# Stacks read from two queues, an output bias added a stage earlier, and filler products on TensorE in a four-layer transformer kernel

## The chip, the cores and the metric

The kernel runs on one core of a Trainium2 chip, as one launch. The metric is the device time in microseconds; 963.40, 967.69 and 969.59 us were measured for the kernel before, so its median is 967.69 us. One execution was also profiled. It took 962.79 us, 961.0 us of them in the span of the profile.

A core has five engines that run their own instruction streams: TensorE (PE; its weight loads are shown as PEld), VectorE (DVE), ScalarE (ACT), GpSimd (POOL) and SyncE (SP). Here SP issues nearly all transfers. The profile also lists the clock that was granted to TensorE, as a share of full speed.

## The reference

1,024 tokens of width 256 pass through four layers. Each layer normalises and adds an attention-like part, then normalises and adds a feed-forward part. All inputs and weights are float32.

```python
x = x + L0_attn(ln(x))      # 16 heads of 16: q, k scaled, rotary, LN; causal softmax; @ Wo + bo
x = x + L0_ffn(ln(x))       # W2 (fwht(silu(x W1) * (x W3))), hidden width 1024
x = x + L1_attn(ln(x))      # 16 heads of 16, biases, causal softmax; @ WO + b
x = x + L1_ffn(ln(x))       # silu(gate) * up, the 2 largest of every 4 kept, down
x = x + L2_attn(ln(x))      # sigmoid gates, tanh values, h[t] = g[t] h[t-1] + v[t]
x = x + L2_ffn(ln(x))       # 8 experts, the best 2 of each token, and a shared expert
x = x + L3_attn(ln(x))      # attention over an axis of few keys; @ wo
x = x + L3_ffn(ln(x))       # ternary weights, silu(gate) * up, RMS norm, down
```

## The kernel before, in words

The tokens lie in 8 tiles of 128 in `m.x` (128 partitions, tile, 256). The program is a row of stages. Each stage is a block of its own with one instruction stream per engine and its own semaphores, and between two stages all five engines meet at a barrier. The stages in order, by the tag in the names of their tiles, with their rough start in the profiled execution: n0 (norm), rotary, s0 (58 us), at0 (79), o0 (216), f0 (237), n2 (318), s1 (328), at1 (352), o1 (490), f1 (507), n4 (601), recurrence (612), n5 (631), f2 (640, experts), n6 (842), single key (850), o3 (878) and f3 (891).

**Norms.** `norm_stage` (L99) computes mean and deviation per tile on VectorE and ScalarE, and TensorE transposes each normalised tile by two products with the identity (L253), each pair waiting for its tile. The transposed halves are copied out of PSUM by ScalarE and VectorE, for n2 and n4 as a high and a low part (L220, L179), for n5 and n6 plain (L224, L183). For n0 the stage waits first for the identity (`ident_ready`). The feed-forward stages f0, f1 and f3 have their norm inside: `HalfNorm` (L1294) turns the first four tiles (`turn`, L1359) ahead of the first products (L1472; in f1 those of `sparse_ffn_stage`), and the other four later.

**Split stage.** q and k must reach the scores as three bf16 parts that stand under each other on the partitions. `split_stage` (L413) makes the parts by units (ScalarE and VectorE), computes V on TensorE (L450) and lets VectorE add V's bias for all 8 tiles on the way into `v_all` (L489). Once a unit is done SP writes it to `scratch` in HBM (L497; semaphore `written[u]`), and `read_stack` (L402) reads it back 16 partitions by 16: six transfers of `qs` for w = 0, six of `ks` for w = 1, all on `m.stacked`. There are four groups of four heads; SP reads group 0 in the split stage, and groups 1 to 3 within the attention (`read_group`).

**Attention.** `attention_stage` (L649) computes in TensorE's products of L705 and L708 (mask) the scores whose maxima VectorE takes (L806), sends the negated maxima as three extra rows into the stack, computes the scores anew, less their maximum (L729), lets ScalarE take the exponential (L786) and multiplies by the values (L745). `order_of_products` (L559) plans, from constants for each engine's speed, in which order TensorE does maxima, scores and values; the result is the list `ORDER`, the same for both attentions. The first entry of kind "values" is number 39 of it, counted from 0.

**Output stage.** `out_stage` (L855) turns `oT` back (L882), takes the reciprocal of the softmax sums (L940), normalises (L942), transposes again (L892), multiplies by the output weights (L900) and adds into `m.x` (L947). At its start VectorE adds the output bias to all of `m.x` (L951) and waits for that. o0 computes, besides, products with a Hadamard matrix for f0's weights. `single_key_stage` (L1937) does projections and transposes on TensorE, then softmax and sums on VectorE into `att`.

**Experts.** f2 opens with 32 gate products of 8 columns (L1038), then come products of the shared expert (L1066) while VectorE sorts out the routing. GpSimd sends the tokens to their slots with 16 indirect transfers (L1285).

## Time and profile before

| | |
|---|---|
| median of 3 runs | 967.69 us (963.40 to 969.59) |
| profiled execution | 962.79 us, span 961.0 us |
| mean granted clock of TensorE | 0.901 |
| PE busy | 797.6 us, 83% of the span (4306 instructions) |
| DVE busy | 624.4 us, 65% (1318) |
| ACT busy | 387.0 us, 40% (655) |
| POOL busy | 153.4 us, 16% (208) |
| moved by DMA | 63.96 MB, mean 67 GB/s |
| costliest groups | maxima of the scores, L806 on DVE: 90.7 us in each attention; exponentials, L786 on ACT: 73.8 us in each |

Busy is time in which an instruction of the engine runs; waiting at a semaphore is idle. A row of the timeline gives the start and the busy time of an instruction (or of several of one kind that follow each other), what it reads and writes, and in brackets how long its engine had been idle before it and what it waited for. "<-PEq L112" means that the engine's own sequencer came last, here at the barrier between stages; "issue" means that no wait is to be seen. Two clocks matter: 1.00 is TensorE at 2.4 GHz, 0.50 at 1.2 GHz.

### The profile page before, as it was taken

How to read it: one execution, taken by the hardware profiler on the slowest of the kernel's cores; microseconds unless marked ns; L12 is line 12 of the kernel's file. 1: busy time of each engine (PE TensorE's matmuls, PEld its weight loads, DVE VectorE, ACT ScalarE, POOL GpSimd, SP SyncE). 2: the span in 40 equal slices, each digit the busy share in tenths (PEclk: the TensorE clock that was granted, in tenths of full speed). 3: DMA queues.
4: the chain of work that ended last, by engine and by line, in shares of the span. 5: the costliest groups of instructions: out<-in, count | busy, mean ns of one | idle time of the engine just before them, and what ended most of it. 6: DMA issues, size and time to landing. Idle time of an engine off the chain costs nothing. (4 is left out here: it accounts for less than half of the span.)

```text
span 961.0 us, 12407 instructions
## 1 busy us (share of the span) xinstructions
PE 797.6 (83%) x4306; PEld 513.8 (53%) x4306; DVE 624.4 (65%) x1318; ACT 387.0 (40%) x655; POOL 153.4 (16%) x208
## 2 busy tenths in 40 slices
PE   6256899987899678999986896669999999478796
PEld 5143344325688553334255786555556666266575
DVE  6887888808774689788346977452267771265764
ACT  3141457683521423666746432541122222043543
POOL 1800121120020001112210000105112221100143
PEclk9666899999899787999998997769999999888798
DMA  6227300000000472200007000993201110310000
GB/s 206 93 81 217 103 2 1 3 2 1 1 1 1 147 246 84 67 3 2 2 1 127 1 1 1 326 375 113 66 28 45 45 45 27 109 45 1 1 23 22
DMA packets 49554, 63.96 MB, mean 67 GB/s; under 512 B 12534, under 2 KB 34806, under 8 KB 49494
## 3 DMA queue, kind: packets, MB, share of 16 engines
q1 hardware_dynamic: 47622, 58.05, 19.7%
q0 software_dynamic: 1872, 5.13, 1.5%
q8 instruction: 35, 0.57, 0.3%
q14 instruction: 25, 0.20, 0.1%
HBM read 50.30 MB, written 15.51 MB: 68 GB/s over the span
## 5 line engine op out<-in xcount | busy, mean ns | idle before, releaser
L806 DVE TENSOR_REDUCE at1mx<-at1ps_s 128x1 f32<-128x512 f32 (+3 forms) x152 | 90.7, 655 | 17.5 <-PE at1ps_s L708 10.4
L806 DVE TENSOR_REDUCE at0mx<-at0ps_s 128x1 f32<-128x512 f32 (+3 forms) x152 | 90.7, 655 | 17.0 <-PE at0ps_s L708 10.0
L786 ACT ACTIVATE at1probs<-at1ps_e 128x1024 f32<-128x1024 f32 (+3 forms) x96 | 73.8, 809 | 45.9 <-PE at1ps_e L729 45.5
L786 ACT ACTIVATE at0probs<-at0ps_e 128x1024 f32<-128x1024 f32 (+3 forms) x96 | 73.8, 809 | 45.5 <-PE at0ps_e L729 45.2
L1070 PE MATMUL f2ps<-gu_raw,f2xT_b 128*128 x184 | 82.9, 593 | 1.0 <-ACT f2xT_b L1145 1.0
L1163 ACT ACTIVATE f2sg<-f2ps 128x512 f32<-128x512 f32 x31 | 18.5, 598 | 134.3 <-PE f2ps L1070 100.9
L705 PE MATMUL at0ps_s<-ks,qs 96*128 96x512 bf16 (+3 forms) x192 | 58.1, 364 | 6.8 <-DMA ks<-scratch 5.3
L705 PE MATMUL at1ps_s<-ks,qs 96*128 96x512 bf16 (+3 forms) x192 | 58.0, 363 | 6.0 <-DMA ks<-scratch 4.4
L1239 DVE TENSOR_TENSOR f2h<-f2sg,f2ps 128x512 f32<-128x512 f32 x31 | 21.3, 686 | 61.6 <-ACT f2sg L1163 42.1
L1070 PEld LDWEIGHTS f2ps<-gu_raw,f2xT_b 128*128 128x128 f32 x184 | 34.8, 190 | 35.5 <-issue 34.4
L729 PE MATMUL at1ps_e<-qs,ks 99*128 99x512 bf16 (+3 forms) x192 | 46.7, 339 | 4.1 <-ACT at1probs L786 2.3
L729 PE MATMUL at0ps_e<-qs,ks 99*128 99x512 bf16 (+3 forms) x192 | 46.7, 339 | 3.9 <-ACT at0probs L786 1.8
L1290 POOL DMA_INDIRECT rows_out<-xT,f2x_in x23 | 29.0, 1259 | 124.8 <-DVE xT L1227 124.8
L795 POOL TENSOR_SCALAR_AFFINE_SELECT at0probs<-at0probs 128x256 f32<-128x256 f32 x64 | 25.8, 409 | 143.0 <-ACT at0probs L786 142.5
L795 POOL TENSOR_SCALAR_AFFINE_SELECT at1probs<-at1probs 128x256 f32<-128x256 f32 x64 | 25.8, 409 | 140.7 <-ACT at1probs L786 140.2
L1098 PE MATMUL f2ps<-dn_raw,xT 128*128 x184 | 43.7, 380 | 1.1 <-DVE xT L1227 1.1
L745 PE MATMUL at0ps_v<-at0probs,v_all 128*32 128x512 f32 (+3 forms) x384 | 41.8, 498 | 0.1
L745 PE MATMUL at1ps_v<-at1probs,v_all 128*32 128x512 f32 (+3 forms) x384 | 41.8, 498 | 0.1
L705 PEld LDWEIGHTS at0ps_s<-ks,qs 96*128 96x128 bf16 x192 | 18.9, 104 | 43.0 <-DVE at0mx L806 28.3
L705 PEld LDWEIGHTS at1ps_s<-ks,qs 96*128 96x128 bf16 x192 | 18.9, 105 | 42.1 <-DVE at1mx L806 28.2
L1098 PEld LDWEIGHTS f2ps<-dn_raw,xT 128*128 128x128 f32 x184 | 33.2, 190 | 5.3 <-issue 1.7
L1708 PE MATMUL f1ps_o<-f1part_dn,f1hpart 128*128 128x256 f32 x192 | 27.7, 312 | 6.5 <-DVE f1hpart L1835 6.5
(400 smaller groups left out, 1772.1 us busy)
## 6 DMA issues: line engine op xcount, KB each, us to landing
gu_raw<-in_L_ffn_w_gate_up SPq DMA_DIRECT2D x8, 1024.0 KB, 12.4
scratch<-parts SPq DMA_DIRECT2D x8, 768.0 KB, 3.8
qs<-scratch SPq DMA_DIRECT2D x48, 128.0 KB, 2.8
ks<-scratch SPq DMA_DIRECT2D x48, 128.0 KB, 2.8
dn_raw<-in_L_ffn_w_down SPq DMA_DIRECT2D x8, 512.0 KB, 12.2
f2x_in<-slots_in SPq DMA_DIRECT2D x23, 129.0 KB, 2.0
slots_in<-in_c_empty SPq DMA_DIRECT2D x1, 2944.0 KB, 17.2
traw<-in_L_ffn_w_gate_up SPq DMA_DIRECT2D x1, 2048.0 KB, 11.6
```

What stands on the lines that cost most here:

```text
L705: ins = pe.matmul(ps_s[:, i % MAX_BANKS, a:a + width], qs[0:STK, g, j + h, qt * P:qt * P + P], ks[0:STK, g, j + h, lo:lo + width], start=T ...
L729: ins = pe.matmul(ps_e[:, v % SCORE_PAIRS, i, 0:n], ks[0:ROWS, g, j, kt * P:kt * P + P], qs[0:ROWS, g, j, lo:lo + n], start=True, stop=True)
L745: ins = pe.matmul(ps_v[32 * j:32 * j + 32, CH - n:CH], v_all[:, g, kt, j, :], probs[:, (s * GH + j) % PROBS, 0:n], start=(kt == 0), stop=( ...
L786: act.activation(probs[:, slots(v), 0:n], ps_e[:, v % SCORE_PAIRS, :, 0:n], ACT.Exp, scale=HD ** -0.5)\
L795: pool.affine_select(pair, pair, [[0, PAIR], [1, P]], ALU.is_ge, 0.0, base=0, channel_multiplier=-1)\
L806: dve.tensor_reduce(mx[:, p % 2, lo // CH, j:j + heads, t], rows_of, AX.X, ALU.max).then_inc(s_red, 1)
L1070: ins = pe.matmul(o, xT_b[:, a % 2, k, :], w, start=(k == 0), stop=(k == KD - 1))
L1098: ins = pe.matmul(ps[:, 6, 0:D], hT[:, b % 2, f, :], w, start=(f == 0), stop=(f == FT - 1))
L1163: act.activation(sg[:, u % 2, :], ps[:, u % 2, :], ACT.Silu).then_inc(sgs, 1)
L1239: dve.tensor_tensor(h[:, u % 2, :], sg[:, u % 2, :], ps[:, 2 + u % 2, :], ALU.mult).then_inc(hs, 1)
L1290: pool.indirect_dma_start(ys[:, :], bass.IndirectOffsetOnAxis(ap=dest, axis=0), y[:, b % YS, :], None)\
L1708: ins = pe.matmul(ps_o[:, c % 2, t, :], hpart[:, a, j, t * P:t * P + P], parts[1][wp][:, blk * 4 + j, :], start=(blk == 0 and j == 0 and t ...
```

## The change

1. **Fillers.** A new `keep_busy` issues `count` bf16 products of the identity by the identity repeated four times (128 x 512) into a PSUM bank that is not in use then; nothing reads them. They stand ahead of and behind the transposes of n2, n4, n5 and n6 (9 and 8), ahead of and behind those of the first half norm in f0, f1 and f3 (9 and 8), at the start of both attentions (6, and one ahead of each of the first 39 entries of `ORDER`), and at the end of the single-key stage (12).
2. **Stack transfers.** Of group 0, SP reads the six of `qs` and two of `ks`; GpSimd reads the other four of `ks`, on a semaphore of their own, both after `written[1]`.
3. **V bias.** For tiles 4 to 7 a product of one row (ones by bias) adds it on TensorE and ScalarE copies the result; VectorE keeps tiles 0 to 3.
4. **Output bias.** VectorE adds it at the end of the attention, not at the start of the output stage.

```diff
+def keep_busy(pe, m, bank, count):
+    for _ in range(count):
+        pe.matmul(bank.rearrange("p (a n) -> p a n", n=P), m.identb[:], m.identb[:].unsqueeze(1).to_broadcast([P, CH // P, P]),
+                  start=True, stop=True)
...
@@ norm_stage, tensor
             if ident_ready is not None:
                 pe.wait_ge(*ident_ready)
+            else:
+                keep_busy(pe, m, ps[:, 7, :], 9)
...
+            if ident_ready is None:
+                keep_busy(pe, m, ps[:, 7, :], 8)
@@ read_stack
-def read_stack(sp, m, g, w):
-    for slot, part in enumerate(PARTS_OF[w]):
+def read_stack(eng, m, g, w, slots=range(NSLOT), signal=None):
+    for slot in slots:
+        part = PARTS_OF[w][slot]
         src = m.scratch[w, part, g * GH * HD:(g + 1) * GH * HD, :].rearrange("(h d) n -> d h n", d=HD)
-        sp.dma_start(m.stacks[w][slot:STK:NSLOT, g, :, :], src).then_inc(m.stacked, 16)
+        eng.dma_start(m.stacks[w][slot:STK:NSLOT, g, :, :], src).then_inc(m.stacked if signal is None else signal, 16)
+BY_SP = 2
+def stacked_by_sp(g):
+    return (g + 1) * STACK_SIGNALS - 16 * (NSLOT - BY_SP)
@@ split_stage
-                                    start=start, stop=stop)
+                                    start=start, stop=stop and t < T // 2)
+                if t >= T // 2:
+                    ins = pe.matmul(ps[:, t, 0:D], m.ones[0:1, :].to_broadcast([1, P]), v_bias[0:1, :],
+                                    start=False, stop=True)
...
+            for t in range(T // 2, T):
+                act.wait_ge(v_full, t + 1)
+                act.activation(v_all[:, :, t, :, 0:HD], heads(ps[:, t, 0:D]), ACT.Copy)
...
-            for t in range(T):
+            for t in range(T // 2):
                 dve.wait_ge(v_full, t + 1)
                 dve.tensor_tensor(v_all[:, :, t, :, 0:HD], heads(ps[:, t, 0:D]), heads(v_bias), ALU.add)
...
-            for w in range(2):
-                sp.wait_ge(m.written[w], 16)
-                read_stack(sp, m, 0, w)
+            sp.wait_ge(m.written[0], 16)
+            read_stack(sp, m, 0, 0)
+            sp.wait_ge(m.written[1], 16)
+            read_stack(sp, m, 0, 1, range(BY_SP))
...
+        @block.gpsimd
+        def _(pool):
+            pool.wait_ge(m.written[1], 16)
+            read_stack(pool, m, 0, 1, range(BY_SP, NSLOT), m.stacked_by_pool)
@@ attention_stage
-                    pe.wait_ge(m.stacked, (g + 1) * STACK_SIGNALS)
+                    pe.wait_ge(m.stacked, stacked_by_sp(g))
+                    pe.wait_ge(m.stacked_by_pool, 16 * (NSLOT - BY_SP))
...
+            keep_busy(pe, m, ps_v[:], 6)
             pe.wait_ge(m.stacked_ones, 16)
-            for kind, n in ORDER:
+            for place_in_order, (kind, n) in enumerate(ORDER):
+                if place_in_order < FIRST_VALUES:
+                    keep_busy(pe, m, ps_v[:], 1)
...
+            dve.tensor_tensor(m.x[:], m.x[:], out_bias.unsqueeze(1).to_broadcast([P, T, D]), ALU.add)
@@ out_stage
-            if bias is not None:
-                b = bias.unsqueeze(1).to_broadcast([P, T, D])
-                dve.tensor_tensor(m.x[:], m.x[:], b, ALU.add).then_inc(biased, 1)
-                dve.wait_ge(biased, 1)
@@ HalfNorm.turn
         if half:
             pe.wait_ge(self.ready, KD)
+        else:
+            keep_busy(pe, m, self.spare, 9)
...
         ins.then_inc(self.turned, 1)
+        if not half:
+            keep_busy(pe, m, self.spare, 8)
@@ single_key_stage
+            pe.wait_ge(copied, len(blocks))
+            keep_busy(pe, m, ps_b[:, 0, :].bitcast(F32), 12)
```

TensorE at the opening of at0, before (L705 scores for the maxima, L708 the mask):

```order
L686 UNCONDITIONAL_BRANCH [waits barrier_Pool_Activation_PE_DVE_SP_release]
L705 MATMUL at0ps_s<-ks,qs 128x128 [waits stacked0,stacked_ones0]
L708 MATMUL at0ps_s<-identb,above 128x128
L705 MATMUL at0ps_s<-ks,qs 128x128
...
L705 MATMUL at0ps_s<-ks,qs 128x256
```

and of the change (L78 is the filler, L738 the product that was L705, L741 the mask):

```order
L718 UNCONDITIONAL_BRANCH [waits barrier_Pool_Activation_PE_DVE_SP_release]
L78 MATMUL at0ps_v<-identb 128x512 x6
L78 MATMUL at0ps_v<-identb 128x512 [waits stacked_ones0]
L738 MATMUL at0ps_s<-ks,qs 128x128 [waits stacked_by_pool0,stacked0]
L741 MATMUL at0ps_s<-identb,above 128x128
...
L78 MATMUL at0ps_v<-identb 128x512
L738 MATMUL at0ps_s<-ks,qs 128x256
```

Seven fillers stand ahead of the first scores, the first six of them ahead of any wait of the stage, and one ahead of each further entry.

SP in s0, before (`written0_1` is `written[1]` of layer 0, `s0_low` counts finished parts):

```order
L497 DMA scratch<-parts 128x3x1024 [waits s0_low] x2
L406 DMA qs<-scratch 16x4x1024 [waits written0_0]
L406 DMA qs<-scratch 16x4x1024 x5
L406 DMA ks<-scratch 16x4x1024 [waits written0_1]
L406 DMA ks<-scratch 16x4x1024 x5
```

and of the change, SP first, then GpSimd:

```order
L522 DMA scratch<-parts 128x3x1024 [waits s0_low] x2
L418 DMA qs<-scratch 16x4x1024 [waits written0_0]
L418 DMA qs<-scratch 16x4x1024 x5
L418 DMA ks<-scratch 16x4x1024 [waits written0_1]
L418 DMA ks<-scratch 16x4x1024
```

```order
L98 ISA x10
L536 UNCONDITIONAL_BRANCH
L418 DMA ks<-scratch 16x4x1024 [waits written0_1]
L418 DMA ks<-scratch 16x4x1024 x3
L442 UNCONDITIONAL_BRANCH
```

Four of the six transfers of `ks` have moved from SP's stream to GpSimd's, which had no work in this stage; the two writes that follow on SP come four issues earlier.

## Rows read from the trace of the kernel before

PE and PEld are TensorE's products and weight loads; in every timeline the columns are those that the group of f0 names.

**Rows 1.** The page, part 2: the granted clock in 40 slices, in tenths.

```profile
PEclk9666899999899787999998997769999999888798
```

**Rows 2.** Stretches: length, busy (count) of PE, PEld, DVE, ACT, POOL, clock, DMA share, GB/s.

```profile
58.30:64.10 5.80, 5.79 (x28) 5.80 (x29) 3.76 (x8) 4.04 (x6) 0.00 (x0) 0.50 0.13 17
64.10:66.00 1.90, 1.90 (x13) 1.75 (x13) 1.87 (x5) 1.48 (x3) 0.00 (x0) 1.00 0.23 77
79.00:84.60 5.60, 5.60 (x31) 3.12 (x32) 4.57 (x9) 0.00 (x0) 0.00 (x0) 0.50 1.00 316
84.60:88.00 3.40, 1.48 (x8) 0.42 (x6) 3.23 (x10) 0.36 (x2) 0.00 (x0) 1.00 0.92 236
88.00:98.20 10.20, 9.54 (x34) 4.15 (x35) 8.66 (x15) 3.24 (x3) 0.82 (x2) 0.50 0.47 146
245.30:248.40 3.10, 3.03 (x7) 2.50 (x8) 2.04 (x9) 1.78 (x4) 0.00 (x0) 0.50 0.00 0
328.20:333.70 5.50, 5.49 (x13) 4.34 (x14) 1.12 (x2) 0.69 (x1) 0.00 (x0) 0.50 0.72 222
334.00:341.50 7.50, 7.50 (x34) 6.03 (x33) 6.93 (x13) 6.23 (x11) 0.00 (x0) 1.00 0.32 110
494.20:497.60 3.40, 3.40 (x12) 2.86 (x11) 1.30 (x4) 0.47 (x2) 0.00 (x0) 0.50 0.00 0
612.20:617.00 4.80, 4.77 (x11) 3.80 (x12) 0.00 (x0) 1.96 (x2) 0.00 (x0) 0.50 1.04 389
878.40:883.20 4.80, 4.69 (x14) 3.59 (x15) 0.42 (x1) 1.15 (x3) 0.00 (x0) 0.50 0.00 0
898.60:903.70 5.10, 5.07 (x16) 4.22 (x17) 1.68 (x6) 2.13 (x5) 0.00 (x0) 0.50 0.00 0
```

**Rows 3.** Timeline, f0: start, length, engine, line, operation, count, [idle before <-releaser].

```profile
241.38 1.85 PE L1359 MATMUL f0ps_o<-ident,n1xn 128*128 128x128 f32 x8 [4.66 <-DVE n1xn L1340]
...
245.37 0.77 PE L1472 MATMUL f0ps_g<-x1hi,f0part_gu 128*128 128x512 f32 x1 [2.15 <-DVE x1lo L1371]
```

**Rows 4.** Timeline, behind the norm n2 and in the norm n6.

```profile
328.21 0.77 PE L440 MATMUL s1ps<-x2hi,wp1hi 128*128 128x512 f32 x1 [2.05 <-PEq L112]
845.13 1.11 PE L253 MATMUL n6ps<-ident,n6xn 128*128 128x128 f32 x4 [17.18 <-DVE n6xn L163]
```

**Rows 5.** Timeline, opening of the MoE stage f2.

```profile
639.56 6.97 PE L1038 MATMUL f2ps<-gate_w,xT 128*128 128x8 f32 x32 [1.03 <-PEq L112]
...
646.38 6.07 PE L1066 MATMUL f2ps<-xT,shared_gu 128*128 128x512 f32 x8
```

**Rows 6.** Timeline, opening of the output stage o3.

```profile
878.46 1.08 PE L892 MATMUL o3ps<-ident,att 128*128 128x128 f32 x4 [4.13 <-PEq L1944]
```

**Rows 7.** Timeline, opening of the output stage o1.

```profile
489.67 2.29 DVE L951 TENSOR_TENSOR x<-x,l1b 128x2048 f32<-128x2048 f32 x1 [22.82 <-PEq L664]
...
492.77 0.44 PE L892 MATMUL o1ps<-ident,o1a_tm 128*128 128x128 f32 x2 [2.03 <-DVE o1a_tm L942]
```

**Rows 8.** Timeline of s0's end and the opening of at0; SPq is SP's DMA queue.

```profile
64.75 3.69 SPq L497 DMA_DIRECT2D scratch<-parts  x2
...
73.10 3.78 SPq L406 DMA_DIRECT2D ks<-scratch  x6
73.75 2.73 DVE L489 TENSOR_TENSOR v_all<-s0ps,l0b 128x256 f32<-128x256 f32 x8
...
78.98 0.27 PE L705 MATMUL at0ps_s<-ks,qs 96*128 96x128 bf16 x1 [5.35 <-DMA ks<-scratch]
```

**Rows 9.** Instructions of line L1285: count, min/median/max ns, first and last start.

```profile
L1285 POOL DMA_INDIRECT slots_in<-xn,f2slot_i x16: 957/961/1174, 655.8 to 675.0; - x16
```

**Rows 10.** The page, parts 5 and 6: busy, mean ns; KB, us to landing.

```profile
L1290 POOL DMA_INDIRECT rows_out<-xT,f2x_in x23 | 29.0, 1259 | 124.8 <-DVE xT L1227 124.8
...
scratch<-parts SPq DMA_DIRECT2D x8, 768.0 KB, 3.8
```

**Rows 11.** Timeline of VectorE in the first scores of at0.

```profile
93.57 3.17 DVE L806 TENSOR_REDUCE at0mx<-at0ps_s 128x1 f32<-128x512 f32 x5 [1.04 <-PE at0ps_s L705]
```

More of the change, by code:

```diff
@@ L854, in out_stage @@
 @stage
-def out_stage(nc, ctx, m, tag, w, w_ready, bias, oT=None, att=None, turned=None):
-    names = ("_tr1", "_norm", "_tr2", "_aT", "_mm", "_res", "_rz", "_had_mm", "_had_b", "_had_v", "_biased")
-    tr1, norm, tr2, aT_s, mm, res, rzs, had_mm, had_b, had_v, biased = (sem(nc, ctx, tag + x) for x in names)
+def out_stage(nc, ctx, m, tag, w, w_ready, oT=None, att=None, turned=None):
+    names = ("_tr1", "_norm", "_tr2", "_aT", "_mm", "_res", "_rz", "_had_mm", "_had_b", "_had_v")
+    tr1, norm, tr2, aT_s, mm, res, rzs, had_mm, had_b, had_v = (sem(nc, ctx, tag + x) for x in names)
     with ExitStack() as tmp:
@@ L1294, with __init__ @@
 class HalfNorm:
-    def __init__(self, nc, own, tmp, tag, room):
+    def __init__(self, nc, own, tmp, tag, room, spare):
         names = ("_sums", "_stats", "_std", "_inv", "_shift", "_xn_v", "_xn_a", "_tr", "_high", "_ready")
@@ L1309, in __init__ @@
         self.warm = sb("warm", [P, 1])
-        self.room = room
+        self.room, self.spare = room, spare
     def tiles(self, half):
@@ L1689, in sparse_ffn_stage @@
         ps_o = tmp.enter_context(nc.psum_tensor(tag + "ps_o", [P, 2, TC, D], F32))
-        nm = HalfNorm(nc, ctx, tmp, norm, ps_o[:, 1].rearrange("p (k t) d -> p k (t d)", k=KD))
+        nm = HalfNorm(nc, ctx, tmp, norm, ps_o[:, 1].rearrange("p (k t) d -> p k (t d)", k=KD), ps_u[:, 1, :])
         block = tmp.enter_context(nc.Block())
@@ L2158, in attention @@
             oT = sb("oT" + layer, [P, GROUPS, N], stack=stack)
-            attention_stage(nc, ctx, m, "at" + layer, v_all, oT)
-            out_stage(nc, ctx, m, "o" + layer, wa[:, :, 3 * D:4 * D], ready, bias, oT=oT, turned=turned)
+            attention_stage(nc, ctx, m, "at" + layer, v_all, oT, bias)
+            out_stage(nc, ctx, m, "o" + layer, wa[:, :, 3 * D:4 * D], ready, oT=oT, turned=turned)
         with ExitStack() as ffn0:
```

12 lines of the change are left out of this document (7 added, 5 removed).

## The prediction, as it stood before the result was known

> **What bounds the kernel now.** I first read the busy shares in 40 slices with the granted clock of TensorE. It is often below full speed, and nearly always where a stage opens [rows 1]. Then I took a table of stretches with their granted clock [rows 2]. Nine stretches show TensorE busy almost without a gap at 0.50, the lower of its two levels (1.2 GHz), and each follows a stretch in which TensorE paused for some microseconds. The price of the low level comes from one stage: in s1 13 products of 512 columns took 5.50 us at 0.50 (0.42 us each), and 34 took 7.50 us at 1.00 (0.22 us). So a stretch in which TensorE is the bound and works at 0.50 gives back about 0.45 of its length at 1.00. Third, the timeline at each edited place says what ends the wait there, and fourth, the rows of the stack transfers say when an attention can begin.
>
> **The change part by part.** One filler is a bf16 product of 128 by 512 columns, so by the s1 pace 0.42 us at the low and 0.22 us at the full clock. There are 9 before and 8 behind the transposes in n2, n4, n5, n6 and in the first half norms of f0, f1, f3; 6 plus 39 in each attention; 12 at the end of the single-key stage: 68 + 51 + 90 + 12 = 221. That is 49 us of new work on TensorE at full clock, 93 us at the low one. It costs nothing where TensorE would wait anyway, so the cover has to be checked place by place.
>
> *Half norms.* In f0 TensorE waited 4.66 us for the first normalised tile; 9 fillers take 2.0 us (low: 3.8), so they fit either way. Eight transposes end at 243.2, the first product starts 2.15 later, at 245.37 [rows 3]: 8 fillers take 1.8 us at the full clock and fit, at the low clock they take 3.4 and make it 1.2 us late. If the clock holds, the 3.1 us at 0.50 that follow [rows 2] give 1.4 us; the first activation waits for them and comes that much earlier. f1 is the same code: 1.4. f3 needs 5.1 us at 0.50: 2.3.
>
> *Full norms.* n2's transposes end 2.05 us before the next stage's first product, which starts at 328.21, released by the barrier [rows 4]. Eight fillers fit (1.8 us in 2.05), and what hides them is the copies out of PSUM on ScalarE and VectorE. s1 then starts at the full clock; its 5.5 us at 0.50 give 2.4. n4 has the same shape, and the recurrence spends 4.8 us at 0.50: 2.2. In n5 and n6 there is less to copy: the gap behind n5's transposes is 1.03 us [rows 5], and n6 has the same code. Eight fillers overrun it by 0.7 at the full clock and by 2.4 at the low one. In n5 the transposes themselves end some tenths earlier at a higher clock, so I take 0.5. n6 comes when TensorE has been idle for 17.18 us [rows 4], so its 9 fillers ahead run at the low clock; I take 0.7 lost. Behind n5 stand 32 gate products of 8 columns, 6.97 us, and then 8 products of 512 columns, 6.07 us [rows 5]. The gate products at the full clock save 3.1. During those 6.97 us of short products the clock did not rise, so I do not count on it to hold through them, and take nothing for the second group (at best 0.45 of it, 2.7 more).
>
> *Single-key stage.* TensorE is done 4.13 us before its next stage starts at 878.46 [rows 6]; 12 fillers take 2.6 us there (low: 5.0, 0.9 late). The output stage spends 4.8 us at 0.50: 2.2.
>
> *Output bias.* The addition of 2048 elements takes 2.29 us. In o1 it stands first, and the first normalisation waits for it: TensorE waits 2.03 us until 492.77 [rows 7]. At the end of the attention VectorE had been idle for 22.82 us, so there it is free. The reciprocal needs the first two tiles' transposes (some 0.7 us of the stage), not the addition: 1.6 saved. In o0 TensorE first multiplies by the Hadamard matrix, which does not need x and hides the addition: 0. With that gap gone the clock should not fall in o1; the 3.4 us at 0.50 give 1.5.
>
> *V bias.* VectorE loses 4 of 8 additions (0.34 us each, 2.73 in all [rows 8]), ScalarE gains four copies, TensorE four one-row products (by the s1 pace 0.42 us each at most). All of it is done before the transfers are: 0. If they were faster, up to 1.4 would show.
>
> *Stack transfers.* SP issues 6 of ks in 3.78 us (0.63 each) behind 6 of qs, the last at 76.2, and the first product of at0 waits for it until 78.98: it lands 2.7 after its issue [rows 8]. GpSimd now sends four of them. The trace has no plain transfer from GpSimd; its 16 indirect ones of L1285 stand 1.28 us apart (0.96 busy) [rows 9], and the 23 of L1290, beside a busier VectorE, are 1.26 busy [rows 10], so about 1.6 apart. Both queues wait for written[1]: its write was issued at about 68.1 (the second of two, done at 68.4 [rows 8]) and such writes land after 3.8 [rows 10], so 71.9 (SP came to it at 73.1 and did not wait). At SP's pace the last of GpSimd's would land at 76.5, 2.5 before now, and SP's own two at 76.4; at 1.28 the last is issued at 75.7 and lands at 78.4, 0.6 earlier; at 1.6 at 79.4, 0.4 later. I take 0.6, the nearest row, per attention.
>
> *Fillers in the attention.* From 79.0 to 98.2 VectorE's maxima set the pace: the longest of its waits for TensorE there is 1.04 us [rows 11]. With the first maximum some 0.4 earlier, a clock that holds gives at most 1.9 in all. TensorE's own work in these 19.2 us was 5.60 + 1.48 + 9.54 = 16.6 us busy, 15.1 of them at 0.50; at the full clock it is half of those and 1.5, 9.1 us, and 39 fillers add 8.6. That is 17.7 in 19.2, but only if the clock is high: each microsecond at 0.50 does half. From 3 us at 0.50 on, the attention can get longer. I take 0.5 saved per attention (bounds: 1.9 saved, 13.8 lost).
>
> **Sum:** 1.4 + 1.4 + 2.3 + 2.4 + 2.2 + 3.1 + 2.2 + 1.6 + 1.5 + 2 × 0.6 + 2 × 0.5 = 20.3 saved, less 0.5 + 0.7: 19.1. The profiled execution took 962.8 us (span 961.0), so 943.7. The three timed runs have their median at 967.7, so against them it is 948.6; the lowest of them was 963.4. I forecast **946**, 2.3 above the sum on the profiled execution, and put the rivals on the same scale.
>
> **A rule against the trace.** From 58.3 to 64.1 TensorE ran nothing but fp32 transposes, 5.79 us busy at 0.50, and from 64.1 it had 1.00 [rows 2]. The Trainium skill, page "TensorE: Matmul & The Clock Gate", section Part 4, says that transposes do not count as activity for the clock gate. The trace disagrees; by that rule the clock would sink in every norm between the two groups of fillers, and the sum would lose what rival A takes away.
>
> **Rivals.** *A. The clock sinks again inside the norms.* For: the tiles arrive slowly, so TensorE is idle for most of the time between the 9 and the 8; against: the fillers behind come at once. Then s1, the recurrence and the gate products keep the low clock for most of their stretch: 19.1 - 7.7 = 11.4 saved, **954**. Chance 0.22.
> *B. GpSimd's transfers are starved.* For: VectorE works almost without a gap there, and GpSimd's transfers beside a busy VectorE took a third longer. If none got out before VectorE ends (75.1 with four additions instead of eight), the last would land at 75.1 + 3 × 1.28 + 2.7 = 81.6, 2.7 late in both attentions in place of 0.6 early: 19.1 - 6.6 = 12.5 saved, **953**. Chance 0.08. The Trainium skill, page "SBUF — State Buffer", section "SBUF: two separate sides", describes this as a trap: GpSimd cannot write descriptors while VectorE holds the shared port.
> *C. Slower: the fillers do not lift the clock.* They are on the order list in front of work, not behind it. If the clock stays at 0.50 in both openings, 39 × 0.42 = 16.4 us stand beside the 16.6 us of own work in 19.2: 13.8 longer each. The other sites then save nothing but 1.6 (bias) and 1.2 (stack), and lose 1.4 at n2, 2 × 2.4 at n5 and n6, and about 4 × 1.2 at the half norms and the single-key stage: 962.8 + 27.6 + 11.0 - 2.8 = 998.6, on the runs' scale **1001**. It decides from 3 us of low clock per opening. Against it: the clock rose after 5.6 us in the opening of at0 as it stands [rows 2]. Chance 0.05.
> *D. No effect.* Most fillers are too early to hold the clock and late enough to cost about what they give; only the bias remains: 1.6 to 6 saved, **963**. Chance 0.08.
>
> **Numbers.** My forecast has 0.57. Its own range, from the bounds above, is 936 to 953; with A and B inside it the range is 935 to 959. About 1% (9.7 us) is what timing this kernel can tell from no change. Faster by over 1% means below 958: the forecast, A and B, less what of their spread passes it, 0.86; within 1% 0.09, nearly all of it D; slower 0.05, C.
>
> **What would show it.** In the changed profile the granted clock is 1.00 when the first products of s1, the recurrence, f0, f1, f3 and o3 start; the reciprocal of o1 starts under 1 us after its stage; fillers end before the barrier in n2 and n4, after it would have come in n6; the first product of an attention waits for a transfer and comes within 1 us of now relative to its split stage; the maxima of the first 20 us have no waits over 0.3 us. I am wrong if the clock is 0.50 in the openings of the attentions for over 6 us, or if the four transfers of GpSimd lie over 1.6 us apart.

## The result, and the profile after

The changed kernel takes 961.19 us (median of 20 runs, 952.67 to 968.09), the kernel before 968.27 us in the same number (963.40 to 971.04): a ratio of 0.9924, 95% interval 0.9909 to 0.9939. It is 0.8% faster, 7.1 us. The forecast was 946 us, 21.7 us below the 967.69 us that the kernel before had then, with a range of 935 to 959; the measured time lies outside it. The ratios here leave out two executions in a slower state, one of the changed kernel (968.09 us) and one of k1 below (1182.67 us).

The profiled execution of the changed kernel took 960.93 us (span 959.1), near its median. That of the kernel before took 962.79, 5.5 below its own median; this matters below. The page of the changed kernel follows; the granted clock is 0.942 on the whole, 0.901 before.

```profile
PE 827.5 (86%) x4543; PEld 516.6 (54%) x4543; DVE 621.5 (65%) x1310; ACT 389.1 (41%) x663; POOL 161.2 (17%) x216
...
PEclk9678899999999999899999998989999999889998
...
L831 POOL TENSOR_SCALAR_AFFINE_SELECT at0probs<-at0probs 128x256 f32<-128x256 f32 x64 | 27.5, 436 | 117.2 <-ACT at0probs L822 116.6
```

The clock row is higher in twelve slices, all of which had 6 to 8 [rows 1], and lower in one. TensorE is busier by 30 us: the 221 fillers add 70 us, and the higher clock takes part of it back. The mean of GpSimd's masks has risen from 409 to 436 ns, but the masks have not become slower one by one. The same line by its instructions (count, min/median/max ns), in the kernel before and in the changed one:

```profile
L795 POOL TENSOR_SCALAR_AFFINE_SELECT at0probs<-at0probs x64: 407/408/442, 94.2 to 214.2; 128x256 f32<-128x256 f32 x64
```

```profile
L831 POOL TENSOR_SCALAR_AFFINE_SELECT at0probs<-at0probs x64: 403/406/2286, 96.7 to 218.9; 128x256 f32<-128x256 f32 x64
```

One mask of the 64 takes 2.29 us; the median is 406 ns. It starts at 197.81, 0.27 us behind the start of the output bias's addition on VectorE (from 197.54, 2.28 us long), and ends 0.27 us behind its end.

Stretches of the changed kernel, columns as in [rows 2]:

```profile
79.10:82.20 3.10, 3.08 (x9) 1.15 (x10) 0.00 (x0) 0.00 (x0) 0.00 (x0) 0.50 1.04 396
82.20:98.20 16.00, 13.98 (x89) 6.98 (x88) 14.02 (x28) 2.58 (x3) 0.41 (x1) 0.99 0.43 124
242.00:246.00 4.00, 2.16 (x10) 0.87 (x10) 3.86 (x21) 3.18 (x7) 0.00 (x0) 1.00 0.00 0
331.30:334.70 3.40, 3.38 (x15) 2.77 (x16) 0.96 (x2) 1.00 (x2) 0.00 (x0) 1.00 1.02 341
493.60:497.00 3.40, 3.02 (x21) 2.58 (x22) 1.95 (x6) 0.77 (x2) 0.00 (x0) 1.00 0.00 0
611.50:615.00 3.50, 3.43 (x8) 2.71 (x9) 0.00 (x0) 1.88 (x2) 0.00 (x0) 0.53 1.06 386
639.90:644.50 4.60, 4.54 (x32) 4.57 (x33) 0.18 (x1) 3.20 (x2) 0.00 (x0) 0.77 1.07 359
644.50:649.60 5.10, 5.10 (x8) 2.28 (x9) 3.29 (x17) 1.49 (x2) 0.00 (x0) 0.54 1.08 363
879.90:883.00 3.10, 2.80 (x11) 2.24 (x12) 0.42 (x1) 0.76 (x3) 0.00 (x0) 0.73 0.00 0
898.00:903.70 5.70, 5.33 (x28) 4.04 (x27) 3.84 (x12) 4.79 (x9) 0.00 (x0) 1.00 0.00 0
```

The clock is at 1.00 at the start of f0, s1, o1 and f3, as forecast. It is not in at0's fillers themselves (0.50), in the recurrence (0.53), in the gate products and the shared products behind them (0.77, 0.54) and in o3 (0.73). f1 opens at 1.00 too, but its eight fillers behind the transposes fell to 0.53 and took 3.40 us.

The end of s0 and the opening of at0, and the first maxima of VectorE:

```profile
72.31 2.30 POOL L418 DMA_DIRECT2D ks<-scratch  x4 [26.26 <-DMA scratch<-parts]
...
73.30 1.23 SPq L418 DMA_DIRECT2D ks<-scratch  x2
...
74.58 1.12 SPq L522 DMA_DIRECT2D scratch<-parts  x2
...
79.12 3.15 PE L78 MATMUL at0ps_v<-identb 128*128 128x512 bf16 x7 [4.61 <-PEq L442]
```

```profile
82.98 6.13 DVE L842 TENSOR_REDUCE at0mx<-at0ps_s 128x4 f32<-128x512 f32 x11 [7.63 <-PE at0ps_s L741]
```

This is the row to read twice. TensorE's first filler starts at 79.12, released by the sequencer at a barrier, not by a transfer, and the seven fillers take 3.15 us at the low clock. The first scores start at 82.06 and VectorE's first maximum at 82.98; before, they were at 78.98 [rows 8] and 80.03.

Lengths of the stages, from the first instruction of each to that of the next (for the attentions from the barrier ahead to the barrier behind; s0 and s1 end at that barrier), in us. The right column is the kernel with the two bias parts alone (k5, below), so a second sight of all stages without fillers. Over the table 2.0 us are saved; the profiled executions differ by 1.9 us (962.79 and 960.93), their medians by 7.1.

| stage | forecast: saved | before | changed | biases only |
|---|---|---|---|---|
| s0 | 0.6 | 20.04 | 20.49 | 20.07 |
| at0 | 0.5 | 137.58 | 141.57 | 138.06 |
| f0 | 1.4 | 80.69 | 79.23 | 81.78 |
| s1 | 2.4 + 0.6 | 23.26 | 21.29 | 22.40 |
| at1 | 0.5 | 138.07 | 140.87 | 137.95 |
| o1 | 3.1 | 17.18 | 13.82 | 13.84 |
| f1 | 1.4 | 94.45 | 93.15 | 94.10 |
| n4 and recurrence | 2.2 | 30.09 | 29.44 | 30.62 |
| n5 | -0.5 | 8.16 | 9.95 | 8.16 |
| f2 | 3.1 | 202.64 | 203.44 | 204.92 |
| n6 and single key | -0.7 | 36.26 | 36.54 | 36.28 |
| o3 | 2.2 | 11.94 | 11.55 | 12.14 |
| f3 | 2.3 | 70.61 | 67.63 | 70.72 |

### The profile page after: what moved, and what is told of

Same layout as the page of the kernel before. It is cut to its first block and busy times, and to the rows that moved or that the text cites. A ratio compares the mean times of both kernels' runs of the same rounds, so it can differ in the third digit from the quotient of the medians.

```text
span 959.1 us, 12876 instructions
## 1 busy us (share of the span) xinstructions
PE 827.5 (86%) x4543; PEld 516.6 (54%) x4543; DVE 621.5 (65%) x1310; ACT 389.1 (41%) x663; POOL 161.2 (17%) x216
## 3 DMA queue, kind: packets, MB, share of 16 engines
q1 hardware_dynamic: 46982, 57.00, 19.7%
## 5 line engine op out<-in xcount | busy, mean ns | idle before, releaser
L842 DVE TENSOR_REDUCE at1mx<-at1ps_s 128x1 f32<-128x512 f32 (+3 forms) x152 | 90.7, 655 | 21.8 <-PE at1ps_s L741 14.2
L738 PE MATMUL at0ps_s<-ks,qs 96*128 96x512 bf16 (+3 forms) x192 | 55.2, 336 | 0.7 <-DVE at0mx L842 0.4
L738 PE MATMUL at1ps_s<-ks,qs 96*128 96x512 bf16 (+3 forms) x192 | 55.0, 335 | 0.7 <-DVE at1mx L842 0.4
L738 PEld LDWEIGHTS at0ps_s<-ks,qs 96*128 96x128 bf16 x192 | 17.9, 99 | 33.3 <-DVE at0mx L842 23.6
L738 PEld LDWEIGHTS at1ps_s<-ks,qs 96*128 96x128 bf16 x192 | 17.8, 98 | 33.3 <-DVE at1mx L842 23.6
## 6 DMA issues: line engine op xcount, KB each, us to landing
slots_in<-in_c_empty SPq DMA_DIRECT2D x1, 2944.0 KB, 18.4
```

The source lines that it names most:

```text
L738: ins = pe.matmul(ps_s[:, i % MAX_BANKS, a:a + width], qs[0:STK, g, j + h, qt * P:qt * P + P], ks[0:STK, g, j + h, lo:lo + width], start=T ...
L842: dve.tensor_reduce(mx[:, p % 2, lo // CH, j:j + heads, t], rows_of, AX.X, ALU.max).then_inc(s_red, 1)
```

## The experiments

All were timed beside the kernel before; each is named by its number here (k1 is the first). For the attentions the table gives, in us from the barrier ahead of each, the start of the first score product, of VectorE's 1st, 41st and 81st maximum, and the next barrier:

| kernel | ratio, 95% interval | at0: scores, 1st, 41st, 81st, next barrier | at1: the same |
|---|---|---|---|
| before | | 0.66, 1.71, 29.48, 61.83, 137.58 | 0.84, 1.89, 29.65, 62.18, 138.07 |
| changed | 0.9924 (0.9909 to 0.9939) | 3.10, 4.02, 32.30, 65.56, 141.57 | 3.10, 3.77, 32.02, 64.88, 140.87 |
| k1 | 0.9942 (0.9923 to 0.9961) | 3.10, 4.20, 33.40, 65.87, 141.88 | 2.35, 3.45, 32.17, 63.23, 139.36 |
| k2 | 0.9920 (0.9897 to 0.9943) | 0.54, 1.64, 31.77, 65.08, 141.09 | 0.38, 1.04, 30.64, 63.47, 139.49 |
| k3 | 0.9906 (0.9875 to 0.9937) | 2.67, 3.77, 31.81, 64.93, 140.93 | 1.45, 2.12, 29.72, 60.75, 136.76 |
| k4 | 0.9892 (0.9864 to 0.9920) | 0.31, 1.36, 28.77, 62.06, 138.06 | 0.31, 1.36, 28.74, 61.59, 137.58 |
| k11 | 1.0035 (1.0010 to 1.0059) | 2.67, 3.52, 31.17, 62.20, 137.96 | 2.67, 3.77, 31.20, 64.07, 139.95 |
| k9 | 0.9818 (0.9795 to 0.9841) | 0.78, 1.44, 28.91, 59.95, 135.98 | 0.36, 1.02, 29.03, 61.96, 138.12 |
| k10 | 0.9794 (0.9767 to 0.9821) | 0.81, 1.47, 29.73, 60.79, 136.97 | 0.48, 1.14, 29.47, 60.53, 136.70 |

**k1, the stacks read by SP alone.** The changed kernel with

```diff
-BY_SP = 2
+BY_SP = NSLOT
...
-        @block.gpsimd
-        def _(pool):
-            pool.wait_ge(m.written[1], 16)
-            read_stack(pool, m, 0, 1, range(BY_SP, NSLOT), m.stacked_by_pool)
```

> The changed kernel, but SP reads all twelve stack transfers of group 0 again; GpSimd issues none. Theory LEAD (the seven fillers ahead of the first scores stand behind the barrier of the stages and cost about 3 us in each attention, whoever reads the stacks): in the changed kernel the barrier before at0 comes at 79.0, in the kernel before at 78.4, so here each attention starts its fillers 0.6 earlier and the whole is 1 us faster than the changed kernel, about 960; first scores still start 3 us behind the barrier. Theory QUEUE (GpSimd's transfers hold the barrier and that alone makes the attentions 4 us longer): the scores start where they did in the kernel before, the fillers are hidden in the wait for the stacks, and the time is about 8 us below the changed kernel, 953.

The attentions stay long (141.88 and 139.36) and the ratio is that of the changed kernel within the intervals; the 1 us that LEAD expected on top cannot be told. QUEUE, that GpSimd's part alone makes them longer, is out; the scores still wait for the fillers.

**k2, k3, k4, fewer fillers in the attention.** The changed kernel without the first of these pieces, without the second, and without both:

```diff
-            keep_busy(pe, m, ps_v[:], 6)
...
-                if place_in_order < FIRST_VALUES:
-                    keep_busy(pe, m, ps_v[:], 1)
```

> The changed kernel without the 6 fillers at the start of each attention (the 39 paced ones stay, so one stands ahead of the first scores). LEAD: the scores start 2.5 us earlier in each attention but at 0.50; the first 5 to 6 us of paced fillers cost 0.42 each, so 1 to 2 us of it is lost again: 2 to 4 us faster in all than the changed kernel, about 958. QUEUE: no change from the changed kernel, 961. Theory PACED (the 39 are the cost): slower than or equal to the changed kernel, since the clock rises later.

> The changed kernel without the 39 paced fillers (the 6 at the start of each attention stay). LEAD: the first scores start 0.4 us earlier, the rest as in the changed kernel if the clock holds: 0 to 1 us faster in all, 960 to 961; if it falls in the opening as in the kernel before, 1 us slower. PACED: 2 to 4 us faster per attention, about 955.

> The changed kernel without any filler in the attentions; GpSimd's reads stay. LEAD and PACED both: the attentions take what they took in the kernel before (136.8 and 137.1 us from their first product to their last), plus or minus 0.3 for the transfers; 6 to 8 us faster than the changed kernel, about 954. QUEUE: the attentions stay at 140 to 141 us, time 961.

Without both the attentions are back at 138.06 and 137.58: in the profiles all fillers together cost 3.5 and 3.3 us there. The table splits this: 2.7 and 2.4 us before the first maximum, 0.9 and 1.1 between the 17th and the 41st, at most 0.2 elsewhere. The executions show less. k4's ratio is 0.0032 lower than that of the changed kernel, 3.1 us, where 6 to 8 us were expected, and the two intervals just overlap. The ratios of k2 and k3 cannot be told from that of the changed kernel, so for them the profiles alone speak.

Without the six leading ones (k2) the first maximum comes 2.4 and 2.7 us earlier, but the paced ones then run at the low clock in the opening, and most of it is given back by the 17th maximum (0.5 and 1.4 us left). My expectation for k2, 2 to 4 us, was right in its kind and too large. Without the paced ones (k3) at0 is 0.6 us shorter and at1 4.1. Of the 4.1, 1.7 come before the first maximum, since the leading fillers met a high clock there (scores at 1.45), and 1.0 between the 17th and the 41st; 0.4 is lost between them. 1.8 come between the 41st and the 81st, behind the last of these fillers: the clock happened to hold there. It held (31.0 to 31.1 us between these two maxima) in 7 of the 26 attentions of all kernels but k10, with and without fillers, and fell (32.3 to 33.3 us) in the others; such a difference of 1.3 to 2.3 us in the length of an attention says nothing of a change ahead of it.

From the 17th to the 41st maximum the attentions take 18.1 us in each of the six with paced fillers (changed, k1, k2), at a granted clock of 1.00. They take 17.0 to 17.4 us in k3 and k4, and 17.0 to 17.8 us in all 22 without paced fillers, at 0.77 to 0.85. So the paced ones cost 0.3 to 1.1 us although they hold the clock. In the profiles both parts cost, then, and what they cost together is not the sum of what each saves when it is taken away alone.

**k11, the leading fillers alone.** The kernel before with one line:

```diff
+            keep_busy(pe, m, ps_v[:], 6)
             pe.wait_ge(m.stacked_ones, 16)
```

> The kernel before, with one thing added: 6 fillers at the start of each attention. The step that is tested is the prediction's own, that fillers there cost nothing because TensorE waits 5.35 us for the stacks. LEAD: only 0.66 us (at0) and 0.84 us (at1) of that wait lie behind the barrier; the 6 fillers take 2.6 us, so the first scores come 2.7 us behind the barrier, 2.0 and 1.8 later than before; some 0.5 of it comes back by the clock in the opening. Each attention is 1 to 2 us longer from barrier to barrier (137.6 and 138.1 before), the time 0.2 to 0.4% above before. Rival, the prediction: scores as before, attention shorter by up to 0.5.

TensorE at the opening of at0:

```profile
79.51 2.72 PE L78 MATMUL at0ps_v<-identb 128*128 128x512 bf16 x6 [4.86 <-PEq L431]
82.02 0.31 PE L712 MATMUL at0ps_s<-ks,qs 96*128 96x128 bf16 x1
```

The wait of 4.86 us now ends at the barrier (PEq), and six fillers stand behind it, in front of the scores, which start 2.67 us after the barrier in both attentions, as LEAD said to the tenth. The kernel is slower than before, and the interval excludes no change. The prediction's step is refuted. (at0 got only 0.4 us longer, since the clock held between the 41st and 81st maximum, 31.0 us against 32.3; at1 1.9.)

**k12, the queue part alone.** The kernel before with the split of the reads and the semaphore, nothing else.

> The kernel before with the queue part of the change alone: GpSimd issues four of the twelve stack transfers of group 0, SP's two writes of the second half follow four issues earlier. Theory QUEUE-NIL (GpSimd issues them 0.5 us apart, but its drain holds the barrier until they have landed, and the two writes of 768 KB now run beside them): the first scores come 20.7 us after the start of s0, as before, plus or minus 0.5; time within 0.2% of before. Rival, the prediction: 0.6 us earlier in each attention, 0.1% faster. Rival 2: the barrier with the drain costs, 0.5 to 1 us later each, 0.1 to 0.2% slower.

```profile
71.36 2.30 POOL L414 DMA_DIRECT2D ks<-scratch  x4 [26.22 <-DMA scratch<-parts]
...
72.38 1.24 SPq L414 DMA_DIRECT2D ks<-scratch  x2
...
73.66 1.12 SPq L512 DMA_DIRECT2D scratch<-parts  x2
...
78.09 0.27 PE L728 MATMUL at0ps_s<-ks,qs 96*128 96x128 bf16 x1 [5.16 <-PEq L438]
```

GpSimd issues its four in 2.30 us, 0.51 to 0.74 apart, about as fast as SP with its 0.64, with VectorE busy for 2.21 us beside it, so the forecast's 1.28 and rival B were both wrong. Yet the scores start at 78.09, 20.53 us after the start of s0 (20.70 before), in at1 23.4 after the start of s1 (24.1 before, 23.2 in k5); the ratio is 0.9988 (0.9971 to 1.0005), no effect that can be told. What took the place of SP's issues: TensorE waits 5.16 us for the barrier, which comes when GpSimd's transfers are in. In the trace of the changed kernel GpSimd's drain at the end of its stage is 5.20 us long. The last of its own four transfers lands at 78.62, the drain ends at 78.83 and the barrier comes at 78.96. In all 14 split stages of the kernels in which GpSimd reads, the drain ends 0.21 to 0.22 us behind the last landing of its own. And the transfers themselves have become slower. From 72 to 80 us, of the changed kernel:

```profile
scratch<-parts SPq DMA_DIRECT2D x2, 768.0 KB, 6.8
...
ks<-scratch POOLq DMA_DIRECT2D x4, 128.0 KB, 3.9
ks<-scratch SPq DMA_DIRECT2D x2, 128.0 KB, 4.8
```

and of the kernel before:

```profile
scratch<-parts SPq DMA_DIRECT2D x2, 768.0 KB, 5.0
ks<-scratch SPq DMA_DIRECT2D x6, 128.0 KB, 2.6
```

The two writes of 768 KB each follow four issues earlier and share the time with the reads, which land after 3.9 and 4.8 us in place of 2.6. That the writes are the cause is likely, not shown: no run moves them back alone.

**k5, the biases alone.** Neither fillers nor GpSimd's reads. The part for the output bias, against the kernel before:

```diff
+            dve.tensor_tensor(m.x[:], m.x[:], out_bias.unsqueeze(1).to_broadcast([P, T, D]), ALU.add)
...
-            if bias is not None:
-                b = bias.unsqueeze(1).to_broadcast([P, T, D])
-                dve.tensor_tensor(m.x[:], m.x[:], b, ALU.add).then_inc(biased, 1)
-                dve.wait_ge(biased, 1)
```

> The kernel before with the two bias parts of the change alone (V bias of tiles 4 to 7 by a product of one row, output bias at the end of the attention); no fillers, SP reads all stacks. In the profile of the changed kernel o1 is 3.4 us shorter, and each attention loses 0.26 us between its last maximum and its last exponential, which theory BIAS puts down to the addition at its end, beside which GpSimd's masks take 436 ns instead of 409. BIAS then expects o1 at 13.8 us with no filler near it, both attentions 0.3 longer from the last maximum on, and 962.5 on the scale of a kernel before of 965.5 (0.997). Rival: o1 owes its 3.4 us to the clock, which the fillers of the attention or of the norms carry into it: then o1 stays above 15.5 us here and the time is within 0.2% of before. LEAD says further that the first scores come 0.5 to 0.9 us behind the barrier, as in the kernel before.

```profile
491.81 0.26 DVE L965 RECIPROCAL o1rz<-o1ps 128x16 f32<-128x16 f32 x1 [21.55 <-PE o1ps L907]
...
492.58 0.44 PE L917 MATMUL o1ps<-ident,o1a_tm 128*128 128x128 f32 x2 [0.37 <-DVE o1a_tm L967]
```

The reciprocal starts 0.67 us after the stage's first product and TensorE waits 0.37 us, not 2.03 [rows 7]; o1 takes 13.84 us without any filler near it. k12 splits this saving by chance: there the addition stands where it stood, TensorE waits 2.03 us, but the clock is at 1.00 all through o1, and the stage takes 15.5 us. So of the 3.4 us about 1.7 are the addition and 1.7 the clock, which the prediction had at 1.6 and 1.5. The ratio is 0.9965 (0.9947 to 0.9982). In the same kernel a wait shows in f2 that the profile of before did not have:

```profile
676.33 1.42 DVE L1241 TENSOR_TENSOR x<-f2ps,x 128x256 f32<-128x256 f32 x4 [4.91 <-remote]
```

VectorE's first addition of the shared expert comes after 4.91 us of idle time, and TensorE waits 2.7 us for the addition. The trace names no instruction for the wait ("remote"), but the code does: the addition waits for the semaphore `used`, which TensorE raises at the end of each set of `shared_dn` products. In the profile of before the signal comes 0.02 us behind the end that the trace gives the fourth set. In all other profiles it comes 3.1 to 4.7 us behind (here the set ends at 671.79 and the signal comes at 676.31), with fillers and without (k8, k10, k11 and k12: 4.3 to 5.0 us of idle time). Why it is late is open. n5 and f2 together take 210.8 us in the kernel before, 213.1 in k5 and 212.6 to 213.9 in k6 to k8, k11 and k12, none of which has fillers in n5. So about 2 of the 5.5 us by which the profiled execution of before lay under its median are there.

**k6 and k8, the norms.** k6 is k4 without fillers in n5 and n6, k8 is k4 without fillers in n2, n4, n5 and n6. The edit of k8:

```diff
-            else:
-                keep_busy(pe, m, ps[:, 7, :], 9)
...
-            if ident_ready is None:
-                keep_busy(pe, m, ps[:, 7, :], 8)
```

> The changed kernel without fillers in the attentions and in n5 and n6. In all five profiles with fillers in n5 the stretch from n5 to n6 takes 211.8 to 213.9 us, in the kernel before 210.8. Theory N5 (fillers in n5 overrun its end by 1.8 us, and the earlier routing only meets a wait in the shared products): n5 takes 8.1 us again, n5 to n6 210.8, 2 to 3 us faster than the kernel without attention fillers alone (k4_no_attention_fillers). Rival: the stall in the shared products (1.4 to 4.5 us) has nothing to do with n5 and comes with any program of this length; then n5 to n6 stays above 211.8.

> The changed kernel without fillers in the attentions and in all four full norms (n2, n4, n5, n6); those of the half norms and of the single-key stage stay. Theory NORMS (fillers in n2 and n4 hold the clock, s1 gains 0.8 us of the 2.4 forecast and the recurrence 0.7 of 2.2, the rest is lost behind other bounds or because the clock falls again in the 3 us before the recurrence): against k6_no_n5_n6 s1 is 0.8 us longer, the recurrence 0.7 to 2 us longer, in all 0.1 to 0.3% slower than k6. Rival: the norm fillers give nothing, k8 equals k6 within 0.1%.

n5 is 8.16 again in k6 and f2 204.81, together 213.0; with fillers 213.4 (changed) and 211.8 to 213.9 in the others. The two sides cancel, and the stall in f2 is no work of n5's: the rival stated for k6 was right, and the 2 to 3 us that N5 expected did not come (0.9877, 0.9853 to 0.9900, against 0.9892 of k4). k8 has s1 at 23.7 us to the barrier, k6 21.7. Over all kernels s1 takes 21.1 to 21.8 us with n2's fillers and 22.4 to 23.7 without, so they are worth some 1 to 2 us. n4's are less certain: with them and a gap behind, the recurrence takes 16.9 us in three profiles (k1, k6, k7), 18.4 in three and 19.7 in k4, and 18.4 to 19.2 without them. The kernels' times do not tell k6 and k8 apart (0.9877 and 0.9893).

**k7, fillers ahead of the barrier.** From k6, with SP reading all, and in the split stage, behind the V products, the lines below. `v_read` is raised when VectorE has taken the first tile of V out of the bank that the fillers write.

```diff
+            pe.wait_ge(v_read, 1)
+            keep_busy(pe, m, ps[:, 0, :], 12 if tag == "s0" else 4)
```

> As k6_no_n5_n6, but SP reads all stacks again, and the split stages end with fillers on TensorE (12 in s0, 4 in s1, behind the V products and ahead of the barrier), so that they lie in the wait for the barrier and not behind it. LEAD: TensorE waits from about 74.6 to the barrier at 78.4 in s0; 12 fillers take 2.6 us at the full clock (5.1 at the low one, then 1 us late). The first scores start within 1 us of the barrier at 1.00, and each attention takes 136.5 to 137.5 us from barrier to barrier: 0 to 1 us less than in the kernel before. Time 0.987 of before. If the clock sinks between the fillers and the scores, the attentions take what they took in the kernel before (137.6 and 138.1).

```profile
75.64 2.76 PE L78 MATMUL s0ps<-identb 128*128 128x512 bf16 x12
79.85 0.22 PE L738 MATMUL at0ps_s<-ks,qs 96*128 96x128 bf16 x1 [1.45 <-DMA ks<-scratch]
```

This is the place at which fillers are free. They run from 75.64 to 78.4, the barrier is not later (20.06 us from the start of s0), and the scores start at the full clock as soon as the transfer is in. The ratio is 0.9846 (0.9823 to 0.9869), a little better than the 0.987 expected. at0 gained nothing (138.01, expected 136.5 to 137.5). at1 is as expected (136.64), but by luck: its clock happened to hold between the 41st and the 81st maximum, and k6, without these fillers, has 135.76. What the fillers ahead of the barrier buy did not last: in at0 the granted clock is 0.50 from 82.6 to 91 us. From the first to the 17th maximum both attentions took 10.5 to 10.6 us, as in the kernel before, where those of the changed kernel, with the paced fillers and the clock at 1.00, took 10.2.

**k9 and k10, gaps filled.** k9 puts 12, 20 and 18 fillers where k7 has 8, 8 and 12 (n2, n4, single key). k10 adds, behind the second row of maxima:

```diff
+                if first <= place_in_order < first + 8:
+                    pe.wait_ge(exp_done, 8 - SCORE_PAIRS + 1)
+                    keep_busy(pe, m, ps_e[:, 8 % SCORE_PAIRS, 0, :], 3 if place_in_order == first + 7 else 1)
```

> As k7_split_fillers, with more fillers where a gap was left behind them: 12 behind the transposes of n2, 20 in n4, 18 at the end of the single-key stage. Theory GAP (the clock falls again in the 2.9 us before the recurrence and the 1.5 us before o3, and where the fillers reach up to the barrier it holds): the recurrence takes 16.9 us in every execution (16.9 to 19.7 so far), o3 9.9 (9.9 or 11.5 so far); 1 to 3 us faster than k7. Rival: no effect, or later barriers where the fillers overrun (n4 to the recurrence over 11.2 us).

> As k9_gaps_filled, with 10 fillers more in each attention, spread over the eight entries behind the second row of maxima, where TensorE waits for VectorE some 29 to 34 us behind the barrier and where the clock falls for 3 to 7 us in nearly every profile. From the 40th to the 80th maximum the attentions took 31.0 us where the clock held and 32.4 to 33.3 where it fell. Theory MIDDLE: 31.0 to 31.5 us in both attentions, 2 us faster than k9. Rival PACED (fillers among the maxima delay VectorE, as the 39 did by 1.0 us between the 16th and the 40th maximum): no faster or slower than k9.

TensorE ahead of the recurrence and of o3 in k9:

```profile
600.62 4.48 PE L78 MATMUL n4ps<-identb 128*128 128x512 bf16 x20
605.39 0.47 PE L1932 MATMUL rec_ps<-x4hi,wp2hi 128*128 128x512 f32 x1 [0.30 <-PEq L119]
```

```profile
865.89 4.05 PE L78 MATMUL one_blocks<-identb 128*128 128x512 bf16 x18
870.23 0.63 PE L926 MATMUL o3ps<-ident,att 128*128 128x128 f32 x4 [0.30 <-PEq L1978]
```

The fillers reach up to the barrier (0.30 us of wait, 2.87 and 1.54 in the changed kernel), the recurrence takes 16.88 us and o3 9.88, in k10 too. k9 lies 2.7 us below k7 by the ratios, inside the 1 to 3 us expected, though the intervals overlap. k10 does the same in the middle of the attention. The same stretch of at1 in k9, then in k10:

```profile
375.50:382.00 6.50, 4.65 (x38) 1.65 (x31) 6.14 (x16) 0.27 (x1) 0.11 (x1) 0.87 0.02 3
382.00:388.00 6.00, 6.00 (x21) 2.11 (x23) 3.46 (x9) 4.12 (x5) 0.00 (x0) 0.57 0.68 199
```

```profile
375.50:382.00 6.50, 5.89 (x48) 2.89 (x41) 6.28 (x16) 0.27 (x1) 0.33 (x1) 1.00 0.02 4
382.00:388.00 6.00, 5.59 (x29) 1.65 (x27) 3.98 (x11) 5.28 (x7) 0.00 (x0) 1.00 0.64 198
```

The clock holds at 1.00 where it fell to 0.57, and from the 41st to the 81st maximum both attentions take 31.06 us, as MIDDLE said; some 0.3 us are lost ahead of that. Two out of two, against 7 of 26 without these fillers, is evidence, not proof. In the profiles the two attentions together are only 0.4 us shorter than in k9, whose at0 had a clock that held anyway. k10 runs at 0.9794 (0.9767 to 0.9821) of the kernel before, 947.76 us in the median, the fastest of all here; against k9 (0.9818, 0.9795 to 0.9841) it is not told apart.

## Why the prediction was wrong

**The step that failed is the cover of the fillers at the start of the attention**, "it costs nothing where TensorE would wait anyway". I read the 5.35 us ahead of at0's first product [rows 8] as a wait for the transfer within the stage. A wait is put down to what came last; only 0.66 us of it lay behind the barrier, and the barrier, held by SP's twelve reads and two writes, was at 78.32. Fillers inside the stage can only begin there. The order of the change shows it (the branch that waits for the barrier, then the six). Price by k11: scores 2.0 and 1.8 us later.

**The paced fillers** did what they were for: from the first to the 17th maximum each attention took 10.2 us in place of 10.6, the 0.5 forecast. They cost 0.3 to 1.1 us from the 17th to the 41st, which was not in the sum. Rival C foresaw a longer attention for another reason, a clock that stays low; it rose after 3.1 us, and the attentions got 4.0 and 2.8 us longer, not 13.8.

**How much of the miss that is.** From profile to profile 19.1 us were forecast and 1.9 came, 17.2 too few. The attentions were to give 1.0 and cost 6.8: 7.8 of it. About 1.2 of these 7.8 is the clock between the 41st and the 81st maximum, which differs from one execution to the next. n5 and f2 were to give 2.6 and cost 2.6, of which 2.3 is the good f2 in the profile of before. The recurrence lacks 1.5, o3 1.8, s0 and s1 1.0 each; f3 gave 0.7 more. The runs put less on the attention: k4, without its fillers, saves 10.4 us by its ratio where the changed kernel saves 7.4. So even with the failed step taken out the forecast would have been too high, by the terms below.

**The signs.** Neither of the two that were to tell me that I am wrong came: the low clock in the opening lasted 3.1 us and not 6, and GpSimd's transfers lay 0.50 to 0.74 us apart and not 1.6. The sign that did tell was the first product of at0, 23.6 us behind the start of s0 in place of 20.7 and released by no transfer.

**Stack transfers**, 0.6 each: nothing (k12). The time between GpSimd's issues was taken twice too long; that its drain holds the barrier until they land was not in the sum. The Trainium skill, page "SBUF — State Buffer", section "SBUF: two separate sides", warns of transfers issued by GpSimd while VectorE runs an operation in a mode that takes both ports. Its trap is not seen here in the issues (0.50 to 0.74 us apart with VectorE busy); whether any of VectorE's operations beside them is of that kind no run here shows.

**Clock terms.** Those with little or no gap behind the fillers held in this pair of profiles: f0 1.5, f1 1.3, s1 2.0, f3 3.0 against 1.4, 1.4, 2.4, 2.3. Over all kernels f0 takes 79.2 to 79.8 us with fillers and 80.7 to 81.8 without, f3 3 to 5 us less with them; f1's gain is not sure (92.5 to 94.5 us with, 94.1 to 96.4 without), as its second group ran mostly at the low clock. The rows of TensorE ahead of s1, and of the recurrence:

```profile
328.35 1.89 PE L78 MATMUL n2ps<-identb 128*128 128x512 bf16 x8
331.32 0.47 PE L460 MATMUL s1ps<-x2hi,wp1hi 128*128 128x512 f32 x1 [1.08 <-PEq L119]
```

```profile
611.57 0.66 PE L1935 MATMUL rec_ps<-x4hi,wp2hi 128*128 128x512 f32 x1 [2.87 <-PEq L119]
```

s1 came with 1.00 behind a gap of 1.08 us. The recurrence, with 2.87, gave 0.7 of 2.2, and o3, with 1.54, gave 0.4 of 2.2. Neither gap decides alone: behind 2.7 to 3.0 us the recurrence had the full clock in three profiles (k1, k6, k7) and lost it in three (changed, k2, k3), and o3 had it in two of the eight with 12 fillers (k1, k4). With the gaps filled both had it in both profiles (k9, k10). Rival A's outcome was thus right for n4 and the single-key stage and wrong for n2; there it was the second gap, not the one between the tiles: the eight fillers behind the transposes ran at the full clock in f0, f3, n2 and n4 (1.89 us). In f1 and n5 (3.40 and 3.08 us) it was the one between the tiles.

**The gate products.** The opening of f2, and what came of it:

```profile
636.58 3.08 PE L78 MATMUL n5ps<-identb 128*128 128x512 bf16 x8
```

```profile
639.96 4.74 PE L1071 MATMUL f2ps<-gate_w,xT 128*128 128x8 f32 x32 [0.30 <-PEq L119]
...
678.23 1.97 PE L1140 MATMUL f2ps<-shared_dn,f2h 128*128 128x256 f32 x8 [2.85 <-DVE x L1253]
```

```profile
676.66 1.42 DVE L1253 TENSOR_TENSOR x<-f2ps,x 128x256 f32<-128x256 f32 x4 [2.96 <-remote]
```

Eight fillers in n5 took 3.08 us, the clock having fallen, and n5 became 1.8 longer, not 0.5. The gate products gained 2.2 of 3.1 (4.60 us to the shared products, 6.82 before). Five of eight kernels without fillers in n5 have 6.82 again (k5 to k8, k11), but k9, k10 and k12 have 4.5 to 5.1, so the clock rises there without them too, for a reason that stays open. What was late next I had not named: VectorE's addition at 676.66, for which TensorE waits 2.85 us. n5 and f2 together gave nothing against k6, where 2.6 were forecast.

**Output bias.** 3.1 forecast, 3.4 measured, and all of it is there without fillers (k5). Its cost of nothing was slightly wrong: one mask of GpSimd takes 2.28 to 2.46 us in place of 0.41, in each attention of all eleven kernels in which the addition has moved, and the last exponential comes 22.73 to 22.91 us after the last maximum, not 22.48. (The expectation of k5 speaks of masks of 436 ns; that is a mean over 63 of the old length and this one.) The Trainium skill, in the section just named, says that a VectorE operation with two inputs in SBUF and a GpSimd operation that reads SBUF exclude each other. The one long mask agrees with it: in all 22 attentions it ends 0.26 to 0.27 us behind the addition, also in k10's at0, where it starts 0.09 us behind the addition's start and not 0.27. With the addition in the output stage (before, k11, k12) no mask is longer than 0.45 us.

**The scale.** The profiled execution of before was a good one of its kind (f2 2.3 us, f0 1.1 us shorter than in k5, and 0.8 in the first stage). The terms were sums of its stretches, so a saving against it does not carry over one to one.

## What to carry to other kernels

Before work is put under a wait, find out which part of the wait lies behind the last barrier: the idle time that a row shows may belong to the stage before, and only work placed there is covered. Fillers that are to hold the clock are safe only if they reach from the last real product up to the next one: behind a gap of 1.5 us the gain was lost here in six of eight profiles. Fillers in the stream that feeds the engine that sets the pace have a price of their own even where they hold the clock, here 0.3 to 1.1 us for 39 of them. Read a mean beside its longest member: one mask of 2.29 us looked like 64 slower ones. A transfer moved to another queue brings that engine's drain to the barrier and lets what stood behind it on the old queue run earlier, into the same DMA engines.
